# A decoder layer with experts: router as four column tiles, residual addition on VectorE, 128-row tails, another order of the last slots

## The reference

```python
ln1_out = _layernorm(hidden_states, ln1_weight, ln1_bias)
...
hidden_after_attn = hidden_states + proj_out
ln2_out = _layernorm(hidden_after_attn, ln2_weight, ln2_bias)
x = ln2_out.reshape(-1, H)
logits = jnp.einsum('th,eh->te', x, router_weight)
gate = jax.nn.softmax(logits, axis=-1)
top_probs, top_idx = jax.lax.top_k(gate, TOP_K)
h_mid = jax.nn.gelu(jnp.einsum('th,ehf->etf', x, moe_w1))
expert_out = jnp.einsum('etf,efh->eth', h_mid, moe_w2)
...
moe_out = jnp.einsum('eth,et->th', expert_out, weights).reshape(S, B, H)
return hidden_after_attn + moe_out
```

## Time and profile before

| | before |
|---|---|
| median of 3 timed runs | 788.13 us (785.64 to 791.9) |
| the profiled execution's own time | 791.32 us |
| its span | 789.6 us |
| PE busy | 628.5 us (80%), 5128 instructions |
| weight loads | 536.9 us (68%) |
| DVE busy | 539.7 us (68%) |
| ACT busy | 391.5 us (50%) |
| POOL busy | 321.0 us (41%) |
| attention stage of the second half, first to last closing addition | 284.4 to 422.8 us |
| first expert tile loaded | from 461.48 us |
| expert stage | to about 727 us |
| closing stage | to 789.6 us |

### The profile page before, as it was taken

How to read it: one execution, slowest core, us unless ns; L and a number is a source line. 1 busy time by engine, 2 the same in 40 slices (tenths; PEclk the granted TensorE clock), 3 DMA queues, 4 the chain that set the end, 5 groups by cost and what they waited for, 6 DMA issues and landing times.

```text
span 789.6 us, 19124 instructions
## 1 busy us (share of the span) xinstructions
PE 628.5 (80%) x5128; PEld 536.9 (68%) x5137; DVE 539.7 (68%) x1853; ACT 391.5 (50%) x923; POOL 321.0 (41%) x439
## 2 busy tenths in 40 slices
PE   4889999999961989999965139999999999997000
PEld 3678998898840667777755128888888888886000
DVE  1337878887855466888884836777777777775772
ACT  1335666656625556666534415555555555553233
POOL 0025777677643002566676722222222222222431
PEclk9989999999985899999976559999999999999555
DMA  6062444344311000111111422222222222221873
GB/s 196 0 177 71 143 133 113 106 138 123 97 28 27 1 2 2 42 56 57 56 56 68 154 91 70 72 80 68 79 68 79 69 80 68 80 68 47 279 245 114
DMA packets 48605, 69.19 MB, mean 88 GB/s; under 512 B 10577, under 2 KB 35281, under 8 KB 48561
## 3 DMA queue, kind: packets, MB, share of 16 engines
q1 hardware_dynamic: 40144, 46.30, 20.1%
q0 software_dynamic: 6480, 17.87, 6.1%
q10 hardware_dynamic: 1936, 4.46, 2.0%
HBM read 40.21 MB, written 24.19 MB: 82 GB/s over the span
## 4 chain that ended last, share of the span: by engine, by line
PE 42%; DVE 11%; DMA 5%; issue 3%; ACT 3%; POOL 3%; SPq 2%; DVEq 0%; POOLq 0%; ACTq 0%
PE half_bank L145 9%; PE half_bank L147 9%; PE half_bank L146 9%; PE half_bank L1856 5%; DMA out_dram<-all_w 3%; PE half_bank L1373 2%; PE half_bank L1837 2%; PE half_bank L1449 2%; POOL dispatched L949 2%; PE half_bank L1361 1%; DVE region_k_diag L1216 1%; ACT all_w L1615 1%; PE half_bank L1460 1%; DVE region_v_turned L1229 1%; DVE region_prob L1244 1%
## 5 line engine op out<-in xcount | busy, mean ns | idle before, releaser
L1675 POOL DMA_INDIRECT results<-all_w_qkv,ex_home x71 | 68.3, 961 | 200.6 <-DVE all_w_qkv L1800 170.5
L1707 ACT ACTIVATE region_hid_hi<-half_bank 128x256 fp32r<-128x256 f32 x142 | 46.9, 381 | 79.3 <-PE half_bank L1856 79.2
L949 POOL DMA_INDIRECT dispatched<-all_xh,all_slot_u x64 | 68.6, 1072 | 34.0 <-DVE all_slot_u L1318 17.4
L145 PE MATMUL half_bank<-region_w_hi,region_hid_hi 128*128 x284 | 81.2, 286 | 1.1 <-DVE region_hid_lo L1792 1.1
L146 PE MATMUL half_bank<-all_w,region_hid_hi 128*128 x284 | 79.7, 281 | 0.0
L147 PE MATMUL half_bank<-region_w_hi,region_hid_lo 128*128 x284 | 79.4, 280 | 0.0
L1694 ACT ACTIVATE all_xh<-half_bank,all_ln_b,all_ln_w 128x128 f32<-128x128 f32 x142 | 57.8, 467 | 21.0 <-PE half_bank L1837 21.0
L1800 DVE TENSOR_SCALAR all_w_qkv<-half_bank,ex_gate 128x256 f32<-128x256 f32 x71 | 34.3, 483 | 48.7 <-PE half_bank L147 48.7
L145 PE MATMUL half_bank<-region_w_hi,region_x_hi 128*128 x142 | 62.9, 443 | 0.7 <-DVE region_x_lo L1785 0.7
L1701 ACT ACTIVATE all_w_proj<-half_bank 128x512 f32<-128x512 f32 x71 | 42.5, 599 | 40.0 <-PE half_bank L147 40.0
L145 PEld LDWEIGHTS half_bank<-region_w_hi,region_hid_hi 128*128 128x128 f32 x284 | 53.3, 188 | 11.3 <-issue 7.8
(11 more groups left out here) (241 smaller groups left out, 1809.3 us busy)
## 6 DMA issues: line engine op xcount, KB each, us to landing
all_xh<-dispatched SPq DMA_DIRECT2D x71, 130.5 KB, 2.1
all_w<-in_moe_w_dram SPq DMA_DIRECT2D x32, 256.0 KB, 3.1
all_w<-results SPq DMA_DIRECT2D x12, 512.0 KB, 6.7
all_resid<-at_x SPq DMA_DIRECT2D x32, 128.5 KB
shared_x_t<-in_x_t_dram SPq DMA_DIRECT2D x16, 256.0 KB, 4.2
at_x_tok<-in_x_dram SPq DMA_DIRECT2D x16, 256.0 KB, 4.3
out_dram<-all_w ACTq DMA_DIRECT2D x6, 512.0 KB
dispatched<-all_tail SPq DMA_DIRECT2D x8, 261.0 KB, 3.3
```

Source lines behind the costliest of these rows:

```text
L145: nc.tensor.matmul(out, a_hi, b_hi, start=(start and i == 0), stop=False)
L949: nc.gpsimd.indirect_dma_start(out=dram["dispatched"], out_offset=bass.IndirectOffsetOnAxis(ap=keep["slot_u"][g % SENDS][:, u, k:k + 1], a ...
L1675: nc.gpsimd.indirect_dma_start(out=dram["results"], out_offset=bass.IndirectOffsetOnAxis(ap=home[par][:, 0:1], axis=0), in_=ym[par], in_of ...
L1707: nc.scalar.activation(hid_hi[par][:, cs, :], p_t[half], ACT.Copy).then_inc(s["hid_high"], 1)
```

## The change

Four edits are made together.

1. `route`: the router weights, padded from 8 to 32 columns, become the stationary operand, and the 128 tokens of each tile stream. Each of the group's four tiles writes its own 32 partitions of one PSUM bank, so the result has experts on partitions. ACT copies it to SBUF (`router_out`, new), and PE turns it back with one transpose (`turn_logits`, new). DVE reads the logits from there.
2. `residual` moves from POOL to DVE, behind `second_statistics`.
3. Tails have 128 rows: one transfer of 130.5 KB for each expert where it was 261 KB, and the table clamps a tile's first row by the count of rows of its expert instead of by its count of tiles.
4. The last slots: PE does `turn_logits` and `count_places` of group 6 ahead of the rows of group 7, and ACT does `gates` of group 6 ahead of `second_rows` of group 7.

```diff
-SEGMENT = TOKENS + 2 * P
+QUARTER = P // 4
+SEGMENT = TOKENS + P
...
-        nc.gpsimd.memset(tail[:, :, :], 0.0).then_inc(done, 1)
+        nc.gpsimd.memset(tail[:, :], 0.0).then_inc(done, 1)
...
-        def residual(g):
-            pool.wait_ge(s["h_ready"], 2 * g + 2)
-            for i in range(2):
-                rows = resid[:, g * NI + 2 * i:g * NI + 2 * i + 2, 0:D]
-                nc.gpsimd.tensor_tensor(rows, rows, h_rows[:, 2 * i:2 * i + 2, :], ALU.add).then_inc(s["keep_done"], 1)
-
         for n in range(1, GROUPS):
             if there(n - 3):
                 scatter(n - 3, range(0, 3))
             root(n - 1)
-            residual(n - 1)
...
-        residual(GROUPS - 1)
...
+        def router_out(g):
+            act.wait_ge(s["router_mm"], g + 1)
+            wait(act, s["logits_mm"], g)
+            nc.scalar.activation(logits_t[:, :], p_r[:, 0:P], ACT.Copy).then_inc(s["logits_t"], 1)
...
                 queries(n + 1, 1)
+            if there(n - 2):
+                router_out(n - 2)
             if there(n):
                 prob_turned(n, 0)
...
         h_turned(GROUPS - 2)
+        router_out(GROUPS - 2)
+        gates(GROUPS - 2)
         second_rows(GROUPS - 1)
-        gates(GROUPS - 2)
         weights.make_high("w1", E - 1)
         weights.make_high("w2", 0)
         h_turned(GROUPS - 1)
+        router_out(GROUPS - 1)
...
+        def residual(g):
+            dve.wait_ge(s["h_ready"], 2 * g + 2)
+            for i in range(2):
+                rows = resid[:, g * NI + 2 * i:g * NI + 2 * i + 2, 0:D]
+                nc.vector.tensor_tensor(rows, rows, h_rows[:, 2 * i:2 * i + 2, :], ALU.add).then_inc(s["keep_done"], 1)
...
                 second_statistics(n - 1)
+                residual(n - 1)
...
         route_slots(GROUPS - 2)
+        residual(GROUPS - 1)
         weights.make_low(dve, "w1", E - 1)
...
-            for u in range(NI):
-                for c in range(C):
-                    ins = nc.tensor.matmul(p_r[:, u * E:(u + 1) * E], xh2_t[:, c, u, :], w_router[:, c, :],
+            wait(pe, s["logits_t"], g)
+            for c in range(C):
+                for u in range(NI):
+                    ins = nc.tensor.matmul(p_r[u * QUARTER:(u + 1) * QUARTER, 0:P], w_router[:, c, :], xh2_t[:, c, u, :],
                                            start=(c == 0), stop=(c == C - 1))
-            ins.then_inc(s["logits_mm"], 1)
+            ins.then_inc(s["router_mm"], 1)
+
+        def turn_logits(g):
+            pe.wait_ge(s["logits_t"], g + 1)
+            nc.tensor.transpose(p_r[:, P:2 * P], logits_t[:, :], ident[:, :]).then_inc(s["logits_mm"], 1)
...
                 turn_rows(n + 2, "x", s["xh1_ready"], xh1)
+            if there(n - 2):
+                turn_logits(n - 2)
             if there(n):
                 outputs(n)
...
         route(GROUPS - 2)
+        turn_logits(GROUPS - 2)
+        count_places(GROUPS - 2)
         turn_rows(GROUPS - 1, "h", s["xh2_ready"], xh2[(GROUPS - 1) % SENDS])
-        count_places(GROUPS - 2)
         route(GROUPS - 1)
+        turn_logits(GROUPS - 1)
         count_places(GROUPS - 1)
...
-            sp.dma_start(dram["dispatched"][bass.ds(row, 2 * P), :].rearrange("(t p) d -> p t d", p=P),
-                         keep["tail"][:, :, :]).then_inc(s["tails_out"], 16)
+            row = sp.value_load(tail_i[0:1, bass.ds(e, 1)], min_val=0, max_val=E * SEGMENT - P)
+            sp.dma_start(dram["dispatched"][bass.ds(row, P), :], keep["tail"][:, :]).then_inc(s["tails_out"], 16)
...
-            steps.chain(V.tensor_tensor(skip_f[:, :], skip_f[:, :], own_f[:, :], ALU.min))
-            steps.chain(V.tensor_scalar(skip_f[:, :], skip_f[:, :], float(P), None, ALU.mult))
+            steps.chain(V.scalar_tensor_tensor(skip_f[:, :], skip_f[:, :], float(P), own_f[:, :], ALU.mult, ALU.min))
```

More of the change, by code:

```diff
@@ L978, in batch_axis_attention @@
     gelu_sample = m.sb("gelu_sample", [P, E])
+    logits_t = m.sb("logits_t", [P, P])
     logits = m.sb("logits", [P, NI, E])
@@ L1747, in tile_table @@
                                         bcast(experts[:, :].unsqueeze(1), wide_shape), ALU.is_equal))
-            for table, out in ((before, skip_f), (n_tiles, own_f)):
+            for table, out in ((before, skip_f), (count, own_f)):
                 steps.chain(V.tensor_tensor(wide[:, :, :], hot_t[:, :, :], bcast(table[:, :].unsqueeze(1), wide_shape), ALU.mult))
```

27 lines of the change are left out of this document (13 added, 14 removed).

## The result

| | before | changed |
|---|---|---|
| median of 20 runs each, on one chip | 788.53 us (784.8 to 791.9) | 794.68 us (790.4 to 797.54) |
| ratio, 95% interval | | 1.0067 (1.0051 to 1.0083) |
| profiled execution, its span | 791.32, 789.6 us | 791.24, 789.4 us |

The change made the kernel slower by 4.0 to 6.5 us; +1.2 us was forecast. The changed one reached the first closing addition of the second half at 278.40 us where the other had 284.41, by a first half in which nothing was changed, and lost that lead again.

What follows compares the result with a forecast made beforehand. A near tie of DVE, ACT and PE was taken to bound each group, SP's tail loop the stage's end. +3.3 (residual) - 1.4 (router, slots) - 0.7 (tails) = +1.2 us on 788.13: 789.3 us, range 783.5 to 794.5.

Steps and rivals of the forecast that it cites:

- order of the last slots: End of the attention stage: group 6's slots about 3.4 us sooner; together with the router -1.4 us, bounds -2 and +1.5.
- The hold-up of POOL: Middle groups: DVE's residual additions delay POOL's root by 0.6 to 0.9 us; +3.3 us over six groups, chance 0.52.
- POOL sits out the DVE addition: Reading of the kernel's end: POOL's steps wait while DVE adds two SBUF inputs, 1.11 and 1.98 us against 0.23 and 1.04.
- That root waited for POOL's scatters, not for DVE: Group 7's root, at 426.40 us before, would still start near 426.2, so router 7 starts at 433.9, not 434.09.
- The last router: Group 7's router at the stage's end, on the path at slow clock: 1.2 to 1.4 us instead of 3.57.
- The tails: SP's eight turns stay, transfers halve; the last takes 2.8 us instead of 3.48: -0.7 us, bounds 0 and -1.4.
- stay off the end, as they start sooner too: POOL's scatters of groups 6 and 7 end near 454 us and do not set the end of the stage.
- the end gains nothing: Rival: router tiles do not overlap, or POOL's scatters end last instead of the tails; 791.4 us, chance 0.14.
- The clock: Rival: PE loses work and the clock falls in one more loop stretch, 5 to 8 us in all; 796 us, chance 0.07.
- From the last root's start to SP's first register load: Sign at the end of the stage: this distance shrinks from 17.4 to about 16.2 us.
- the change touches one stage only: Starting point: only the batch-axis attention with the router, about 284 to 443 us, and the gap before the experts were examined.
- Everything else ... lies beside other work: 0: Shorter table arithmetic, less memory set to zero and a wider router weight load cost or gain nothing: 0 us.

Runs made afterwards that it cites:

- a_noresid12: Changed kernel with the residual addition back on POOL and 12 already satisfied waits on PE ahead of the expert stage; 0.9968 of the kernel before.
- after_pads140: Changed kernel with 140 already satisfied waits on PE and 18 on DVE ahead of the expert stage; 0.9964 of the kernel before.
- b_tails: Kernel before with the 128-row tails alone; 0.999 of the kernel before.
- b_tails_router12: Kernel before with the 128-row tails, the new router with its result turned back, and 12 satisfied waits on PE; 0.9993 of the kernel before.
- b_resid: Kernel before with the residual addition alone moved to DVE, behind the second statistics; 1.0028 of the kernel before.
- before_heads20_25: Kernel before with 11 satisfied waits on PE and 5 on DVE ahead of the expert stage; one execution, expert-loop turn 7.167 us.
- after_late140: Changed kernel with 140 and 18 waits on PE and DVE, and the groups' residual addition later on DVE, behind the picking; 1.0041 of the kernel before.

## Why the forecast was right and wrong

That the time would move by less than 1% was right, and so was the mechanism of most terms; the size was not. 789.3 was forecast, 794.68 measured, 5.4 us above it and 0.2 above the range's end; 0.4 of the 5.4 is the kernel before, whose median over 20 runs is 788.53. The terms, in us:

| term | forecast | measured | by |
|---|---|---|---|
| residual, in the groups | +3.3 | +3.7 | a_noresid12, after_pads140 |
| residual, at the end | 0 | -2.1 | the same |
| router | 0 in the groups | -0.25 there, -0.7 at the end | b_tails, b_tails_router12 |
| order of the last slots | -1.4 with the router | -1.8 | b_tails_router12, a_noresid12 |
| tails | -0.7 | -0.8 | before, b_tails |
| place of the two loops | not seen | +5.4 | before, changed |
| one more piece of program | not seen | +1.5 | before, changed |
| sum | +1.2 | +5.0 | measured 4.0 to 6.5 |

Each measured term is one trace against another; the tails' stands across two chips, and the router's in the groups is within what equal kernels differ by. On the chip of the result the groups are 2.9 us longer, not 3.7.

- *The hold-up of POOL* was right in kind and size: the root is 0.57 us later, the forecast had 0.6 if POOL slips in and 0.9 if not. It does slip in, and pays 0.27 and 0.29 us in its two steps. So "POOL sits out the DVE addition", read from the earlier trace rows, does not hold for the second step here. The closing addition's waits changed from DVE to ACT as the trace was to show. That DVE would be ready sooner and that this would be worth nothing was right too.
- *"That root waited for POOL's scatters, not for DVE"*: this step failed, and it is the term that was missed at the end. POOL's additions for group 6 stood in that queue too, so their move brings the root forward. Without them the root of group 7 starts 0.16 us behind its statistics (422.05 and 421.89) instead of 1.36, and 0.21 in b_resid. The end gains 2.1 by it; how the 0.9 beyond the root's 1.2 come about was not followed.
- *The last router*: 1.08 us busy where 1.2 to 1.4 were taken, at half clock; copy 0.29 where 0.47, turn 0.47 where 0.35 were taken.
- *The tails*: the last lands in 2.02 us in the changed kernel, under the 2.8 that was taken and the 2.3 that was estimated; in b_tails, where scatters still run beside it, it lands in 2.77, as taken, and there the term is met. The estimate of 2.3 stands on a fit that the Trainium skill ("DMA: Bandwidth & Descriptors", section "Anatomy of one DMA") states for transfers issued by GpSimd; the tails are issued by SP.
- *The scatters of groups 6 and 7 "stay off the end, as they start sooner too"* holds only with the new order. In b_tails_router12 they end last, which is the rival "the end gains nothing" in part.
- *The clock*: granted at 1.00 from 256 to 402.7 us in the changed kernel's trace. The rival's 796 lies near the measured time for another reason.
- *From the last root's start to SP's first register load* 16.2 us were forecast and 15.35 measured (422.05 to 437.40), 17.4 before.
- *"... the change touches one stage only" and "Everything else ... lies beside other work: 0"* failed, and it decides. The expert stage was never opened, since no line of it is on a changed path. The edit does not touch that stage, it moves its code: 23 instructions on PE and 15 on DVE stand ahead of the loops that did not before. That made each of PE's 33 turns 0.16 us longer (5.4 us from first to last load) and put the fetch of a piece of program behind the last turn (1.5 us).

Two errors offset one another in part: 3.3 us too little gain at the end and 6.9 us of loss unseen. That the time stayed within 1% is owed in part to this, which was luck. Without the second the change is a gain of 0.36% (after_pads140), 2.8 us.

## What to carry to other kernels

When an edit adds instructions ahead of a loop that runs many turns, compare the loop's turn before and after, not only the stages edited; 0.16 us in a turn of 7.2, 33 times, was more than all four edits together. Measure such an edit a second time with some idle waits ahead of the loop, in time in which the engine waits anyway: if the time moves, the place of the code was measured and not the edit. If a gain depends on which of several things ends last, as that of the tails and of the order did here, measure it in the kernel in which the others are out of the way too. When work leaves an engine, ask of each thing queued behind it, also in the last turns, where the queue is another one than in the loop.

## What the runs showed of the hardware

- The programs are fetched in pieces, 16 KB each in PE's queue and 8 KB in the others'. At 64 bytes an instruction (PE's compiled program has 6374 in 407,936 bytes, labels among them) these are 256 and 128 instructions. The two late places are 62 and 64 short of a multiple, as would fit some 60 instructions of start-up code ahead. With it PE's next piece begins at 6338: the program of before ends at 6333, and the kernels looked at that end past it, from 6344 on, fetch one piece more, 25 where before has 24. In before_heads20_25, which ends at 6344, it comes at 796.3 us, behind everything, and the way out stays at 10.57 us. The start-up code is inferred, the places are measured.
- The Trainium skill ("Advanced Engine Details and Errata", section "ISA Cache") states cache lines of 16 KB, 256 instructions, two of them, in 32 KB (128 KB on TensorE), configurable for each engine. For PE the pieces in the trace agree; for the other engines they are 8 KB here. How many are held at a time no run here shows.
- What a boundary inside a loop costs: nothing if the loop's head stands 22 or more instructions ahead of the boundary (five cases); 0.156 us a turn on PE and 0.11 on DVE if it stands 4 to 18 ahead (five cases). Why the distance decides is not shown. That what lies behind the boundary is asked for some 20 instructions ahead, and a branch to a nearer place comes too late for it, would fit; no run tests it.
- A fetched piece takes time of a DMA engine: 1.28 us at 723.0 us, and the scatter it met there landed 1.5 us later than its like in the kernel before (3.88 and 2.41 us from issue). Six kernels fetch a piece at that place, and their scatter there lands in 3.4 to 4.4 us.
- SP's instructions can stand 0.70 us apart, for 11 us in after_late140 and for fewer of them in the other kernels on chips A and C, in its loop over the tails. The cause is open.
